# Four orders changed in a fused graph layer: SyncE's stores, two early loads, one edge step, one block's preparation

## The chip, the cores and the metric

The kernel runs on one core of a Trainium2 chip. The metric is the device time of one launch in microseconds (us), here always of the whole program. PE is TensorE, DVE is VectorE, ACT is ScalarE, POOL is GpSimd, and SP is SyncE, which here issues most DMAs. Each engine works through its own instructions in the order in which they are written; semaphores tie the engines together.

## The reference

One layer on N = 6250 nodes with 256 features and E = 206250 edges sorted by their target. Three terms are added to x, and a mixture of experts follows:

```python
xn = layernorm(x)
# graph attention, 8 heads of 32, 4 edge types
feat = xn @ W_n
el, er = einsum('nhd,hdt->nht', feat, attn_l), einsum('nhd,hdt->nht', feat, attn_r)
e = (sum_t(el[src] * mask) + sum_t(er[dst] * mask) + sum_t(em * mask)) / 3
e = where(e > 0, e, 0.2 * e)
a = exp(e - segment_max(e, dst)[dst]); a = a / segment_sum(a, dst)[dst]
gnn = segment_sum(feat[src] * a[:, :, None], dst)
# linear attention over the nodes
q = softmax(q, -1) * scale; k = softmax(k, over nodes)
mix = layernorm_gamma((q @ (k.T @ v)) @ Wout)
x = x + gnn + mix
# 8 experts, each three layers of 256 x 256
w = softmax(mean over batch of xn2 @ Wr + br)      # xn2 = layernorm(x), batch of 1
h = relu(bn(xn2 @ W1[e] + b1)); h = relu(bn(h @ W2[e] + b2)); y = h @ Wo[e] + bo
x = x + sum_e w[e] * y[e]
```

## The kernel before

There are three phases, each a block of the five engines' programs that ends with a barrier.

**The node phase** works on 49 tiles of 128 nodes. It makes the table of features (256 values and 32 logits of each node) that the edges gather from, and the linear attention. POOL first stores the table, then gathers the rows of 26 edge groups (PRE) ahead of the edge phase (`gather_ahead`, L440): each group is eight indirect gathers into one of two halves of `stage`, and a half is free again when SP has stored it (`ahead_out`). SP stores a gathered group with `store_ahead(i)` (L366), which waits for the group's gathers. Its order is written out by hand: the first 11 groups (FIRST_BESIDE), then for each of the seven chunks c of x one group and one `reload(c)` (L378, 896 KB of x, again needed for the residual), then the output loop. There DVE's `finish` (L683) writes output tile t to one of four buffers of `kexp`, and needs the store of tile t - 4 to have landed; SP's `store_mix` (L371) stores it, three tiles later in SP's own count. After tiles t = 5, 11, ..., 47 of SP's count comes one more `store_ahead`, from number EARLY = 18 on. The last store is `store_er` (L382, 1.2 MB), and SP then waits for all landings (L398).

**The edge phase** has 202 groups of 1024 edges, walked in 250 visits (a group beside a target tile), two visits to a step, so steps k = 0 to 124 (K = 125) and two more to drain. POOL gathers the source rows (L972), eight gathers to a group, and tells the group as `ready` when the gathers have landed, four gathers into the next group or at the end. In step k PE turns the logits of k (`turn_logits`, L1302), makes one-hot transposes and edge terms of k + 1, sums the messages of k - 1 (`segment_sums`, L1325, of which the second visit's last five chunks come at the end of the step), adds the gathered terms of k + 1 (`source_terms`, L1292, the only part that waits for `ready`) and turns the running maxima of k (`turn_maxima`, L1312). In step k DVE does two scans of k (L1181, L1186), `logits` of k + 1 (L1108), `differences` of k (L1192, L1194), `over_terms` and `leak` of k + 1 (L1122, L1126), the selection for k + 2, then `absent` (L1130) and the new maxima of k - 1, which need both segment sums of k - 1, and last the messages of k (L1173). SP loads the edge data of step k + 4 and stores the sums. Two loads for the FFN's block 0, `xm` (L945) and `am` (L946), are issued at step K - 1 = 124 of SP's program.

**The FFN phase** has 13 blocks of four or three node tiles and eight experts (x = 0 to 7). `block_of` sets one order for PE, ACT and DVE: in column x come `up` of x + 1, `middle` of x, `down` of x - 1 and one part of the next block's preparation. Its parts are: 0, normalise the sums, add the residual, statistics (DVE); 1, the deviation (ACT) and xn (DVE, L1699 and L1702); 2, transposes (PE, L1796) and a copy (ACT); 3, the router's matmuls (PE, L1804); 4, the router's logits and the splitting of xnT into two parts (DVE); 5, exp (ACT) and the weights (DVE); 6, transposes of the weights (PE, L1810) and their copy wT (DVE, L1739); 7, the bias matmuls (PE, L1816) and the start of y (DVE, L1744). Every fp32 matrix is used as a high and a low part, so each product is three matmuls (L1822 to L1824), and DVE splits h after each relu (L1653, L1655). In block 0 ACT and DVE also split the weights of each expert as they arrive (`cast_weight`, L1588; `weight_rest`, L1659: one rest in `up`, two in `middle`), and the preparation of block 0's own parts 5 to 7 stands in columns 0 and 1.

Of the kernel before, what the change touches and what calls it, by code (L numbers as in the profile page):

```python
# [42 lines left out]
K = V // 2  # L43
SLOTS = 4
GSLOTS = 7
NEAR = 8
PRE = 26
EARLY = 18
FIRST_BESIDE = 11
REST_AFTER = 1  # L50
RESTS = 1
# [15 lines left out]
B = 4  # L67
# [113 lines left out]
def phase_nodes(nc, io, scr, kept_on):  # L181


    with ExitStack() as ctx:
# [129 lines left out]
        def _(sp):  # L314
# [69 lines left out]
            for i in range(FIRST_BESIDE):  # L384
                store_ahead(i)
            for c in range(NT // XC):
                store_ahead(FIRST_BESIDE + c)
                reload(c)
            turns = dict(zip(range(5, NT, 6), range(EARLY, PRE)))
            tiles(sp, (store_mix, 3), unrolled=True, at={t: partial(store_ahead, i) for t, i in turns.items()})  # L390
# [412 lines left out]
def phase_edges(nc, io, scr, kept_on, opening):  # L803


    with ExitStack() as ctx:
# [40 lines left out]
        opening_in = sem("g_opening_in")  # L847
# [55 lines left out]
        def _(sp):  # L903
# [34 lines left out]
            for k in range(SLOTS):  # L938
                loads(k, k)
                if k == 0:  # L940
                    sp.dma_start(idx[:, :], io["src"][:, NEAR * C:]).then_inc(idx_in, 16)

            def load_first_sums():

                sp.dma_start(opening.xm[:, :, :], scr["xmix"][0:B].rearrange("a p c -> p a c")).then_inc(opening_in, 16)  # L945
                sp.dma_start(opening.am[:, :, :], scr["acc"][0:B].rearrange("a p c -> p a c")).then_inc(opening_in, 16)  # L946

            assert (G - 1) + (B - 1) < 2 * (K - 4)

            def step(k, s):  # L950
                if isinstance(k, int) and k == K - 1:
                    load_first_sums()
                if not known(k, 3):
                    store(k - 3, (s + 1) % 2, 1)
                if not (isinstance(k, int) and k + SLOTS >= K):
                    loads(k + SLOTS, s)
                if not (known(k, 2) or isinstance(k, int) and k >= K + 2):
                    store(k - 2, s % 2, 0)
# [122 lines left out]
        def _(dve):  # L1081
# [123 lines left out]
            def step(k, s):  # L1205

                q = s % 2
                alive = not (isinstance(k, int) and k >= K)
                more = not (isinstance(k, int) and k + 1 >= K)
                joining = not known(k, 2)  # L1210
# [6 lines left out]
                    dve.wait_ge(runm_ok, k + 1)  # L1217
                if joining and not (isinstance(k, int) and k >= K + 2):
                    join(k - 2, q, 0)
                if more:  # L1220
                    logits(k + 1, (s + 1) % SLOTS)
                if alive:
                    differences(k, s)
                if more:
                    over_terms(k + 1)
                    leak(k + 1)
                if choosing:
# [20 lines left out]
                if alive:  # L1248
                    messages(k, s, 0, at[0])
                    messages(k, s, 1, at[1])  # L1250

            over_terms(0)
            leak(0)
# [3 lines left out]
        def _(pe):  # L1257
# [79 lines left out]
            def step(k, s):  # L1337
# [15 lines left out]
                    turn_one_hot(k + 1, s1, 1)  # L1353
                if summing:
                    segment_sums(k - 1, s0, 1, range(0, BEFORE))
                if more:
                    source_terms(at, groups)
                if alive:
                    turn_maxima(k, s)
                if summing:  # L1360
                    segment_sums(k - 1, s0, 1, range(BEFORE, C))

# [3 lines left out]
def phase_ffn(nc, io, scr, kept_on, opening):  # L1366
# [4 lines left out]
    with ExitStack() as ctx:  # L1371
# [93 lines left out]
        def halves(n):  # L1465

            return -(-n // 2)

        SHORT = NB * B - NT
        FULL = NB - SHORT  # L1470
        assert SHORT == 3 and FULL % 2 == 0 and FULL * B + SHORT * (B - 1) == NT
# [5 lines left out]
        def blocks(eng, prepare, up, middle, down):  # L1477
# [4 lines left out]
            def block_of(b, s, n, following):  # L1482
                opening = isinstance(b, int) and b == 0
                for x in range(X):
                    if x < X - 1:
                        up(b, s, n, x + 1)
                    elif following:
                        up(b + 1, 1 - s, following, 0)
                    if opening and x < 2:
                        prepare(0, 0, B, 5 + x)  # L1490
                    middle(b, s, n, x)
                    if opening and x == 1:
                        prepare(0, 0, B, 7)
                    if x > 0:
                        down(b, s, n, x - 1)
                    elif not (isinstance(b, int) and b == 0):
                        down(b - 1, 1 - s, B - 1 if isinstance(b, int) and b > FULL else B, X - 1)
                    if following:
                        prepare(b + 1, 1 - s, following, x)

            for x in range(3):
# [466 lines left out]
```

## Time and profile before

| | |
|---|---|
| median of 3 runs | 3161.24 us (3158.49 to 3166.12) |
| the profiled execution | 3170.54 us, its span 3168.9 us |
| PE busy | 2874.6 us, 91% |
| DVE busy | 2638.7 us, 83% |
| POOL busy | 1852.1 us, 58% (all of it before the FFN) |
| ACT busy | 1700.9 us, 54% |
| node phase | to about 367 us |
| edge phase | to about 2257 us |
| FFN phase | the rest |

The shares are means over three phases with different limits, so no one of them tells what an edit is worth. The four edits lie in short stretches: the output loop (263 to 367 us), the last steps of the edge phase (2150 to 2257 us) and block 0 of the FFN (2257 to 2370 us). For each, the timeline of the engines is read together with what ended the idle time before an instruction. Times are us from the span's start.

### The profile page before, as it was taken

Reading aid. Unit: us, or ns where it says so; the run is one execution under the profiler, and the core shown is the slowest. Engines: PE = TensorE matmul, PEld = TensorE weight load, DVE = VectorE, ACT = ScalarE, POOL = GpSimd, SP = SyncE. Lnnn points to the kernel's source line nnn. Section 1 sums busy time; section 2 is a strip of 40 time slices with the busy share of each in tenths; the row PEclk is TensorE's granted clock in tenths of the full one; section 3 lists DMA queues with packets and bytes.
Section 4 is the critical chain, followed back from the end, with each engine's and each line's share of the span. In section 5 each row is a group of like instructions: output and inputs, shape, how many; then the busy total and the mean of one; then the engine's idle time right before and its main releaser. Section 6 shows DMA issues by size and latency. Waiting matters only on the chain. (4 is left out here: it accounts for less than half of the span.)

```text
span 3168.9 us, 76579 instructions
## 1 busy us (share of the span) xinstructions
PE 2874.6 (91%) x21350; PEld 2376.5 (75%) x21351; DVE 2638.7 (83%) x4799; ACT 1700.9 (54%) x5754; POOL 1852.1 (58%) x3341
## 2 busy tenths in 40 slices
PE   8996589998999999999899999898599999999999
PEld 5565377776777777777777777776388888888899
DVE  5676698998999998899999999898587777777776
ACT  5552256665666665666666666665543333333343
POOL 3888688888888888888888888887000000000000
PEclk9998899999999999999999999999799999999999
DMA  8678867676776767676667676665211000000000
GB/s 312 211 252 298 307 193 202 202 208 197 206 212 199 208 195 197 199 206 199 203 196 205 199 207 206 199 203 156 76 52 34 21 22 21 22 21 18 18 23 10
DMA packets 275943, 500.38 MB, mean 158 GB/s; under 512 B 80679, under 2 KB 177474, under 8 KB 269008
## 3 DMA queue, kind: packets, MB, share of 16 engines
q0 software_dynamic: 85456, 282.69, 30.8%
q1 hardware_dynamic: 190336, 215.88, 21.4%
q8 instruction: 69, 1.13, 0.1%
q14 instruction: 82, 0.67, 0.1%
HBM read 410.81 MB, written 87.57 MB: 157 GB/s over the span
## 5 line engine op out<-in xcount | busy, mean ns | idle before, releaser
L972 POOL DMA_INDIRECT gat<-scratch_table,idx x1360 | 1323.6, 973 | 239.0 <-issue 229.9
L1325 PE MATMUL ps_s<-msg,oh 128*128 128x272 f32 x4000 | 1029.0, 406 | 106.0 <-ACT tmp L1038 55.9
L1325 PEld LDWEIGHTS ps_s<-msg,oh 128*128 128x128 f32 x4000 | 742.7, 193 | 255.5 <-ACT tmp L1038 107.6
L1047 ACT ACTIVATE acc<-acc,sc 128x33 f32<-128x33 f32 x2000 | 458.8, 340 | 224.2 <-DVE acc L1161 222.3
L1610 ACT ACTIVATE h<-ps_h,fsh,fsc 128x512 f32<-128x512 f32 (+1 forms) x416 | 291.1, 751 | 508.8 <-PE ps_h L1824 508.8
L1173 DVE TENSOR_TENSOR msg<-gat,ps_m 128x2048 f32<-128x2048 f32 x250 | 559.3, 2277 | 0.0
L1563 POOL DMA_DIRECT2D out<-y x13 | 9.9, 759 | 897.2 <-DVE y L1778 897.2
L1038 ACT ACTIVATE tmp<-ps_s,sc 128x33 f32<-128x33 f32 x2000 | 386.7, 305 | 17.2
L1027 ACT CAST oh<-ps_o 128x1024 f32<-128x1024 bf16 x250 | 259.3, 1037 | 139.2 <-PE ps_o L1264 137.7
L1653 DVE CAST h_hi<-h 128x1024 fp32r<-128x1024 f32 (+1 forms) x208 | 137.2, 660 | 201.9 <-ACT h L1610 201.8
L1186 DVE TENSOR_TENSOR_SCAN runm<-penr,ps_e 16x1024 f32<-16x1024 bf16 x125 | 284.3, 2274 | 12.8
L1181 DVE TENSOR_TENSOR_SCAN ps_e<-penr,ps_e 16x1024 f32<-16x1024 bf16 x125 | 284.5, 2276 | 2.0 <-PE ps_e L1302 2.0
L1655 DVE TENSOR_TENSOR h_lo<-h,h_hi 128x1024 fp32r<-128x1024 f32 (+1 forms) x208 | 242.1, 1164 | 7.2
L440 POOL DMA_INDIRECT stage<-scratch_table,pidx x208 | 205.2, 987 | 43.6 <-issue 41.3
L1822 PE MATMUL ps_y<-w_hi,h_hi 128*128 128x256 f32 x784 | 219.8, 280 | 1.7 <-DVE y L1778 1.7
L1823 PE MATMUL ps_y<-w_lo,h_hi 128*128 128x256 f32 x784 | 220.0, 281 | 0.0
L1824 PE MATMUL ps_y<-w_hi,h_lo 128*128 128x256 f32 x784 | 219.7, 280 | 0.0
L1032 ACT ACTIVATE sc<-dd 128x16 f32<-128x16 f32 x250 | 60.2, 241 | 294.7 <-DVE dd L1155 294.7
L144 POOL MEMSET rest_e<- 128x16 f32 x1408 | 203.7, 145 | 0.4
L1292 PE MATMUL ps_z<-gat,ident 128*128 x500 | 136.8, 397 | 55.6 <-POOLq L992 54.3
L1278 PEld LDWEIGHTS ps_z<-er3e,ohT 128*128 128x128 bf16 x6000 | 168.6, 96 | 18.2 <-issue 0.3
L1264 PE MATMUL ps_o<-identb,ohT 128*128 128x128 bf16 x2000 | 153.7, 220 | 27.3 <-DVE ohT L1101 25.9
(224 smaller groups left out, 5319.8 us busy)
## 6 DMA issues: line engine op xcount, KB each, us to landing
d16r<-scratch_dst SPq DMA_DIRECT2D x250, 256.0 KB
scratch_acc<-acc SPq DMA_DIRECT2D x250, 136.0 KB
scratch_ahead<-stage SPq DMA_DIRECT2D x26, 1152.0 KB, 4.8
gat<-scratch_ahead POOLq DMA_DIRECT2D x26, 1152.0 KB
edge<-in_edge SPq DMA_DIRECT2D x250, 88.0 KB
gat<-scratch_table,idx POOLq DMA_INDIRECT x1360
scratch_table<-stage POOLq DMA_DIRECT2D x49, 144.0 KB, 5.3
xq<-in_xT SPq DMA_DIRECT2D x7, 896.0 KB, 11.4
```

The costliest lines, as they stand in the source:

```text
L972: pool.indirect_dma_start(out=gat[:, s, c, :], out_offset=None, in_=scr["table_rows"], in_offset=bass.IndirectOffsetOnAxis(ap=rows[:, at:a ...
L1027: act.copy(oh[:, s, j, :, :], ps_o[:, 0:C, :]).then_inc(oh_ok, 1)
L1038: act.mul(tmp[:, j, cols], ps_s[j][:, cols], sc[:, j, 1, h:h + 1]).then_inc(tmp_ok, 1)
L1047: act.mul(acc[:, new, cols], acc[:, old, cols], sc[:, j, 0, h:h + 1]).then_inc(scaled, 1)
L1173: dve.tensor_tensor(m4[:, :, :, 0:DH], gat[:, row_of(at), :, 0:D].rearrange("p a c (h d) -> p (a c) h d", h=H), ps_p.rearrange("p (c j h) ...
L1181: dve.tensor_tensor_scan(ps_e[0:2 * H, 0:GE], penr[:, s, 0:GE], ps_e[0:2 * H, 0:GE], NEG, ALU.add, ALU.max).then_inc(runf_ok, 1)
L1186: dve.tensor_tensor_scan(runm[:, ::-1], penr[:, s, GE:0:-1], ps_e[0:2 * H, GE - 1::-1], NEG, ALU.add, ALU.max).then_inc(runm_ok, 1)
L1325: last = pe.matmul(ps_s[j][:, 0:SUMS], oh[:, s, j, c, :], msg[:, 2 * (s % 2) + j, c, :], start=(c == 0), stop=(c == C - 1), skip_group_che ...
L1610: act.activation(hid[:, m, 0:n * P], ps_h[2 * layer + m][:, 0:n * P], ACT.Relu, bias=sh[:, layer, x * KD + m:x * KD + m + 1], scale=sc[:, ...
L1655: dve.tensor_tensor(lo, whole, hi.bitcast(F32), ALU.subtract).then_inc(parts, 1)
L1822: pe.matmul(out, a_hi, b_hi, start=start, stop=False)
L1823: pe.matmul(out, a_hi, b_lo, start=False, stop=False)
```

## The change

- SyncE's stores around the output loop: EARLY is 17. The last chunk's `reload(6)` is no longer preceded by a group's store; group 17 is stored in the output loop after t = 5, groups 18 to 24 after t = 11 to 47, and group 25 after the loop, ahead of `store_er`.
- The early FFN loads: `xm` is issued at step K - 4 = 121 of SP's program, behind the last edge loads and store of step 120, and `am` at step K = 125.
- Step K - 2 = 123 of the edge phase: DVE does `logits`, `over_terms` and `leak` of step 124 at the end, after the messages; PE turns the maxima of step 123 ahead of `source_terms`, while the last five chunks of the segment sums stay behind both.
- Block 1's preparation, which runs in the columns of block 0: part 0 in column 2 (it was in 0), 1 and 2 in column 3, 3 in column 4, 4 in 5, 5 in 6, and 6 and 7 in column 7. Later blocks keep one part to a column.

```diff
@@ -45,7 +45,7 @@
 GSLOTS = 7
 NEAR = 8
 PRE = 26
-EARLY = 18
+EARLY = 17
 FIRST_BESIDE = 11
 REST_AFTER = 1
 RESTS = 1
@@ -384,7 +384,8 @@
             for i in range(FIRST_BESIDE):
                 store_ahead(i)
             for c in range(NT // XC):
-                store_ahead(FIRST_BESIDE + c)
+                if FIRST_BESIDE + c < EARLY:
+                    store_ahead(FIRST_BESIDE + c)
                 reload(c)
             turns = dict(zip(range(5, NT, 6), range(EARLY, PRE)))
             tiles(sp, (store_mix, 3), unrolled=True, at={t: partial(store_ahead, i) for t, i in turns.items()})
@@ -940,15 +941,20 @@
                 if k == 0:
                     sp.dma_start(idx[:, :], io["src"][:, NEAR * C:]).then_inc(idx_in, 16)
 
+            def load_mixed():
+
+                sp.dma_start(opening.xm[:, :, :], scr["xmix"][0:B].rearrange("a p c -> p a c")).then_inc(opening_in, 16)
+
             def load_first_sums():
 
-                sp.dma_start(opening.xm[:, :, :], scr["xmix"][0:B].rearrange("a p c -> p a c")).then_inc(opening_in, 16)
                 sp.dma_start(opening.am[:, :, :], scr["acc"][0:B].rearrange("a p c -> p a c")).then_inc(opening_in, 16)
 
             assert (G - 1) + (B - 1) < 2 * (K - 4)
 
             def step(k, s):
-                if isinstance(k, int) and k == K - 1:
+                if isinstance(k, int) and k == K - SLOTS:
+                    load_mixed()
+                if isinstance(k, int) and k == K:
                     load_first_sums()
                 if not known(k, 3):
                     store(k - 3, (s + 1) % 2, 1)
@@ -1205,6 +1211,7 @@
             def step(k, s):
 
                 q = s % 2
+                closing = isinstance(k, int) and k == K - 2
                 alive = not (isinstance(k, int) and k >= K)
                 more = not (isinstance(k, int) and k + 1 >= K)
                 joining = not known(k, 2)
@@ -1217,11 +1224,11 @@
                     dve.wait_ge(runm_ok, k + 1)
                 if joining and not (isinstance(k, int) and k >= K + 2):
                     join(k - 2, q, 0)
-                if more:
+                if more and not closing:
                     logits(k + 1, (s + 1) % SLOTS)
                 if alive:
                     differences(k, s)
-                if more:
+                if more and not closing:
                     over_terms(k + 1)
                     leak(k + 1)
                 if choosing:
@@ -1248,6 +1255,10 @@
                 if alive:
                     messages(k, s, 0, at[0])
                     messages(k, s, 1, at[1])
+                if closing:
+                    logits(k + 1, (s + 1) % SLOTS)
+                    over_terms(k + 1)
+                    leak(k + 1)
 
             over_terms(0)
             leak(0)
@@ -1353,10 +1364,13 @@
                     turn_one_hot(k + 1, s1, 1)
                 if summing:
                     segment_sums(k - 1, s0, 1, range(0, BEFORE))
-                if more:
+                closing = isinstance(k, int) and k == K - 2
+                if more and not closing:
                     source_terms(at, groups)
                 if alive:
                     turn_maxima(k, s)
+                if closing:
+                    source_terms(at, groups)
                 if summing:
                     segment_sums(k - 1, s0, 1, range(BEFORE, C))
 
@@ -1466,6 +1480,7 @@
 
             return -(-n // 2)
 
+        OPENING = [(), (), (0,), (1, 2), (3,), (4,), (5,), (6, 7)]
         SHORT = NB * B - NT
         FULL = NB - SHORT
         assert SHORT == 3 and FULL % 2 == 0 and FULL * B + SHORT * (B - 1) == NT
@@ -1495,7 +1510,10 @@
                         down(b, s, n, x - 1)
                     elif not (isinstance(b, int) and b == 0):
                         down(b - 1, 1 - s, B - 1 if isinstance(b, int) and b > FULL else B, X - 1)
-                    if following:
+                    if opening:
+                        for part in OPENING[x]:
+                            prepare(1, 1, B, part)
+                    elif following:
                         prepare(b + 1, 1 - s, following, x)
 
             for x in range(3):
```

## Rows read from the trace of the kernel before

**Rows 1.** Timeline, SP's DMA issues: start us, us, queue, line, operation, out<-in, count

```profile
263.73 0.32 SPq L366 DMA_DIRECT2D scratch_ahead<-stage  x1
...
274.32 0.32 SPq L366 DMA_DIRECT2D scratch_ahead<-stage  x1
...
275.19 3.51 SPq L371 DMA_DIRECT2D scratch_xmix<-kexp  x3
...
356.25 0.33 SPq L366 DMA_DIRECT2D scratch_ahead<-stage  x1
...
361.76 0.43 SPq L382 DMA_DIRECT2D scratch_er<-er  x1
```

**Rows 2.** Timeline, DVE in the output loop; the brackets: idle before, releaser

```profile
284.64 0.48 DVE L683 SCALAR_TENSOR_TENSOR kexp<-mixo,rstd,ktile 128x256 f32<-128x256 f32 x1 [14.63 <-DMA scratch_xmix<-kexp]
```

**Rows 3.** Timeline, POOL, the last gather of the node phase

```profile
352.60 0.96 POOL L440 DMA_INDIRECT stage<-scratch_table,pidx  x1 [0.18 <-issue]
```

**Rows 4.** Views of lines 398 and 366, whole run: SP's last waits; landings of group stores

```profile
L398 SPq EVENT_SEMAPHORE  x3: 28/847/2948, 362.2 to 366.1; - x3
...
DMA to landing us min/median/max: 4.1/4.8/6.3
```

**Rows 5.** Timeline, SP, the first of the two early FFN loads

```profile
2204.08 0.43 SPq L945 DMA_DIRECT2D xm<-scratch_xmix  x1
```

**Rows 6.** Timeline, POOL, the last gather of the edge phase

```profile
2203.55 0.95 POOL L972 DMA_INDIRECT gat<-scratch_table,idx  x1 [0.18 <-issue]
```

**Rows 7.** Timeline, PE, steps 123 and 124 of the edge phase

```profile
2210.49 2.07 PE L1292 MATMUL ps_z<-gat,ident 128*128 x4 [8.44 <-POOLq L992]
...
2213.45 4.17 PE L1325 MATMUL ps_s<-msg,oh 128*128 128x272 f32 x10
...
2217.46 1.04 PE L1302 MATMUL ps_e<-ident,e 128*16 128x128 f32 x8
...
2221.18 5.31 PE L1325 MATMUL ps_s<-msg,oh 128*128 128x272 f32 x22 [2.68 <-DVE msg L1173]
...
2228.04 0.64 PE L1312 MATMUL ps_m<-ident,runm 16*128 16x16 f32 x8 [1.55 <-DVE runm L1186]
```

**Rows 8.** Timeline, DVE, steps 123 and 124 of the edge phase

```profile
2212.60 0.75 DVE L1108 TENSOR_TENSOR zm<-ps_z,edge 128x256 f32<-128x256 f32 x2 [9.18 <-PE ps_z L1292]
...
2213.97 0.68 DVE L1122 TENSOR_REDUCE lg<-zm 128x128 f32<-128x512 f32 x1
...
2223.24 2.28 DVE L1181 TENSOR_TENSOR_SCAN ps_e<-penr,ps_e 16x1024 f32<-16x1024 bf16 x1
```

**Rows 9.** Windows: us, busy by engine, then PEclk, DMA share, GB/s

```profile
2206.50:2207.00 0.50, 0.00 (x0) 0.00 (x0) 0.00 (x0) 0.00 (x0) 0.00 (x0) 0.51 0.46 134
```

**Rows 10.** Timeline, PE, block 0 of the FFN

```profile
2300.55 1.22 PE L1816 MATMUL ps_t<-bo_parts,wT 96*128 96x256 f32 x4 [7.30 <-DVE wT L1739]
...
2306.16 0.39 PE L1822 MATMUL ps_h<-fxnT_hi,w_hi 128*128 128x512 f32 x1
...
2314.57 1.04 PE L1796 MATMUL ps_t<-ident,fxn 128*128 128x128 f32 x8
...
2323.87 1.84 PE L1804 MATMUL ps_t<-wr,fxnT 128*128 128x8 f32 x16
```

**Rows 11.** Timeline, DVE, block 0 of the FFN

```profile
2292.25 0.18 DVE L1671 TENSOR_SCALAR rs<-am 128x32 f32<-128x32 f32 x1
...
2297.08 0.38 DVE L1686 BATCH_NORM_AGGREGATE fmv<-fst 128x2 f32<-128x6 f32 x4
...
2307.36 1.39 DVE L1702 TENSOR_SCALAR fxn<-x,fmv,fsd 128x256 f32<-128x256 f32 x4
...
2313.54 0.69 DVE L1653 CAST h_hi<-h 128x1024 fp32r<-128x1024 f32 x1 [0.34 <-ACT h L1610]
...
2315.41 1.29 DVE L1659 TENSOR_TENSOR w_lo<-w_raw,w_hi 128x512 fp32r<-128x512 f32 x2
...
2316.61 1.65 DVE L1778 SCALAR_TENSOR_TENSOR y<-ps_y,w,y 128x256 f32<-128x256 f32 x4
```

## The prediction

> **What bounds the kernel now.** The three phases stand one behind another, so I read each place that the change touches by itself: the page's slices to see the phases, then the waits of each stretch, the timeline of each engine there, and the granted clock. The node phase ends with SP's queue: stores of gather groups, stores of output tiles and one last store share it, and its end is 366.1 us [rows 1, 4]. The edge phase's last steps are one chain through TensorE (PE) and VectorE (DVE), fed by POOL's gathers. In the FFN, PE is the bound once block 0 is past; inside block 0 it waits for DVE once, until 2300.55 [rows 10].
>
> **Part 1, the order of SyncE's stores.** Before, SP issues reload 5 right after the store of group 16 (issued 263.73), then waits for gather group 17 (274.32), and only then come reload 6 and the first output tile's store (275.19) [rows 1]. DVE stands 14.63 us, until 284.64, for that store to free its buffer [rows 2]. After, reload 6 and output stores 0 to 2 go ahead of group 17's store, so store 0 is issued near 265 instead of 275.2. It has two reloads and a group store in front of it on the DMA rings and lands, by the 9.4 us that the old one took behind one of each, some 10 to 12 us later: 275 to 277.5. DVE thus runs 7 to 9 us ahead. That gain doesn't reach the end of the phase. POOL's gathers run without a break and end at 352.60 + 0.96 = 353.56; the store of the last group goes out at 356.25 [rows 1, 3], and that is a floor. In the new order this store comes behind all output stores, and the store of er behind it. Before, er's store goes out at 361.76 and the phase ends at 366.1, 4.3 us later [rows 1, 4]. After, both go out at 356.3 and 356.7; a group's store lands 4.8 us after issue [rows 4], and er's bytes (as many again) behind it need about 3 us: 364.1. Gain 2.0 us. Against it: group 17's store now has reload 6 in front, and gather group 19 waits for it. Before, it had some 2 us to spare (274.32 + 5 against the start of group 19 near 281.3, counted back from 353.56 by seven groups of 10.3 us, eight gathers of 0.96 us with their gaps and fills each); reload 6 in front costs 0 to 3.5 us of landing, so POOL loses 0 to 1.5 us, and all that follows on POOL with it. I take 0.8. **Part 1: -1.2 us**, bounds -3 (the rings clear faster than 4.8 us a store) to +2 (POOL loses 3.5 and only 1.5 is saved).
>
> **Part 2, the early FFN loads.** xm (512 KB) and am (544 KB) are issued from 2204.08 on, while POOL's last gather is issued at 2203.55 and over by 2204.5 [rows 5, 6]. PE waits until 2210.49 for it (8.44 us idle) [rows 7]: 5.9 us from issue to use. In the node phase the last gather of group 25 was in use 356.25 - 353.56 = 2.7 us after issue [rows 1, 3]. Without the two loads beside it I take 2.7 us: ready at 2207.2, 3.2 us sooner. xm now goes out behind step 120's loads, near 2167, beside gathers of that time; each group's landing is awaited by POOL only after four more gathers (5 us), and even the 5.9 us seen here would cost POOL 0.9 us, so 0 to 0.9, taken 0. am goes out after the last loads, near 2228, ahead of the store of visit 245; nothing needs either before the phase's end, 26 us later. No cost.
> The Trainium skill says in DMA: Bandwidth & Descriptors, section Queues, rings and completion order, that each DMA engine takes turns between the queues it has work for. By that rule two busy queues halve each other; the trace agrees (5.9 against 2.7 us). It speaks against the earlier xm as well: gathers beside it would take twice as long, which by the four gathers' margin is still hidden.
>
> **Part 3, the last step but one.** In step 123 PE now turns the maxima before it waits for the gathers, and DVE puts logits, over_terms and leak of step 124 behind the messages. What is queued where decides. PE's remaining segment sums of visit 245 are still behind source_terms, and DVE's absent() still waits for those sums, ahead of the messages. So the wait for the gathers reaches the messages as before, less only the 0.96 us that turning the maxima took between them. The row: source_terms 2210.49, sums from 2213.45 for 4.17 [rows 7]; so from ready to the end of the sums 7.1 us, after 6.2. From the end of the sums to the next scan DVE takes 2223.24 - 2217.62 = 5.6 us [rows 7, 8]. New on the path behind that: logits 0.75, over_terms 0.68 and the short leak, with gaps 1.8 us [rows 8], then PE's turning of the logits, 1.04 us at near full clock [rows 7] and up to 2.1 at half. Before, all of it lay beside the sums, hidden.
> The clock: in PE's idle time, which began at 2202.0, the granted clock was at 0.51 by 2206.5, the level of 1.2 GHz [rows 9], so source_terms took 2.07 us and ten matmuls 4.17, against 22 in 5.31 at full clock (0.24 each) [rows 7]. Now the pause is some 3.5 us, from the maxima near 2203.7 to 2207.2, and then there is a second one of over 7 us, while DVE does messages and logits. I take the low clock for both: 2207.2 + 6.2 = 2213.4 sums; + 5.6 = 2219.0; + 1.8 = 2220.8; turning 1.8 = 2222.7. PE then has 22 matmuls of step 123 that ran before 2226.5 [rows 7] and now start at 2222.7: ten at 0.42 and twelve at 0.24, 7.1 us, to 2229.8; the scans (4.7 us) end earlier, 2227.4. The maxima of step 124, before at 2228.04 [rows 7], come at 2229.8, and the rest of the phase is one chain from there. **Parts 2 and 3: +1.8 us.** Bounds: the clock still up at 2207.2 gives sums at 2210.9, maxima at 2227.3, -0.7; the gathers no sooner than before gives +5.0, with POOL's 0.9 +5.9. Alone, part 2 would have given some -5 and part 3 takes it.
>
> **Part 4, block 1's preparation.** DVE's part 0 runs from 2292.25 to 2297.46, 5.2 us, ahead of the copy of wT for which PE waits until 2300.55 [rows 10, 11]. Moved behind, PE goes on at 2295.5: -5.1. The pause shrinks from 7.3 to 2.3 us, so the down matmuls keep the full clock: the matmuls from 2300.55 to 2306.16 took 5.6 us [rows 10], at full clock 3.3, another -2.3. So up(3) starts at 2298.8, 7.4 us sooner.
> Then the work comes back. PE needs 8.41 us for a weight column x (2306.16 to 2314.57) [rows 10] and would reach the transposes, now at the end of x = 3, after two columns, at 2298.8 + 16.8 = 2315.6. They need part 1 from DVE, and DVE works in order through all of its x = 2 and x = 3 first. That is twice: two splits of 1.87 (2313.54 to 2315.41), three weight rests of 0.6 (two from 2315.41 to 2316.61), four updates of y in 1.6 [rows 11], 7.2 us; and once part 0 with 5.2 and part 1 with 1.6 (1.39 and its reciprocal) [rows 11]: 21.2 us. It can start when ACT hands over the first relu of x = 2, 4.5 us after up(3) starts (2.8 of matmuls, 1.4 of relu, hops): 2303.3, and it waits 0.5 us for the other relu: 2325.0. So PE waits 9.4 us, and comes back at half clock. Place by place: up(5) started at 2306.16 + 16.8 + 0.8 for the transposes + 1.7 for the router's matmuls (2323.87) [rows 10] = 2325.5. Now: 2325.0 + 1.5 for slow transposes = 2326.5, +1.0; the router's 1.7 are still to come, +1.7; and up(5) itself at half clock, by the 2.3 us saved above less the transposes' 0.7, +1.6. At the end of x = 7 parts 6 and 7 stand together: after middle(7) DVE needs ACT's relu 1.5, the split 1.87, four y updates 1.6 and the copy of wT 0.6, 5.7 us with hops, while PE has 2.8 of down matmuls and 0.45 of transposes: it waits 2.5 before the bias matmul, where before a whole column lay between. In all +1.0 + 1.7 + 1.6 + 2.5 = 6.8; less 0.3 for a short old wait for a weight rest. **Part 4: +6.5 us.** Bounds +3 (half the second wait hidden) to +9 (the clock falls in the 2.3 and 2.6 us pauses too). Other loads: am and xm of block 2 wait for part 0, 14 us later than before and still 60 us early.
>
> **Sum.** -1.2 + 1.8 + 6.5 = +7.1 us, on an execution of 3170.54 us (span 3168.9): 0.22%. The same on the median of 3161.24 gives 3168.3. That execution is 9 us above the median; nothing above depends on it.
>
> **Rivals.**
> 1. DVE keeps up in block 0 (the not slower side). If part 0 found free time on DVE in column 2, PE would wait at the transposes only for the last y updates and part 1, 2.7 us, at full clock, and part 4 would be -7.4 + 2.7 + 2.5 = -2.2: total -1.6, 3159.6. It decides at 16.8 us of PE against 21.7 of DVE. For it: DVE has idle pieces in the old columns (0.34 before 2313.54) [rows 11]. Against: the count above leaves it none. 0.13.
> 2. The clock is up at 2207.2: -0.7 instead of +1.8, total +4.6, 3165.8, no difference that can be told. For it: the pause is shorter than the 4.5 us in which the clock fell. 0.17.
> 3. The 14.63 us stall was on the path: the phase ends with DVE, 6 us sooner. Against: the floor at 356.25. -6 instead of -1.2: 3163.5. 0.08.
> 4. The change doesn't do what it says with the gathers: they land as late without the loads. +5.0 instead of +1.8: 3171.5. Against: they share the rings from 2204.5 to 2210.5. 0.15.
> The forecast 0.42; the rest, POOL's loss and falls of the clock in the short pauses, 0.05, above it.
>
> **Chances.** About 0.2% (6.3 us, 3167.6) is what can be told from no change. The forecast lies just over it: three quarters of its case slower. Slower 0.49, same 0.43, faster 0.08 (most of rival 1's and 3's lower ends). The range for 8 in 10: 3161.0, between rivals 1 and 3, to 3174.0, rival 4 with part 4's upper bound.
>
> **What would show it.** Output loop: DVE's wait shrinks to some 5 us, and POOL's last gather ends at 353.6 to 355; the edge phase starts under 2 us sooner. Step 123: source_terms near 3 us sooner after the last gather, a PE gap of 7 us before the logits are turned, half clock after it. Block 0: bias matmul 5 us sooner, a gap of 9 us before block 1's transposes, one of 2 to 3 before its bias matmul. Wrong if no such 9 us gap is there, or if the node phase is shorter by over 4 us.

## The result

The changed kernel takes 3169.42 us (median of 11 runs, 3166.18 to 3176.59); the kernel before, measured beside it, takes 3161.24 us (3157.93 to 3167.98). The ratio is 1.0027, with a 95% interval from 1.0018 to 1.0036: 8.5 us slower, between 5.7 and 11.4. The prediction was 3168.3 us. All medians are over all launches; the ratios leave out the few launches that were far slower than their fellows.

The profiled execution's span is 3174.9 us, where the one of before is 3168.9. The busy times of the page hardly move, so the stretches have to be read one by one. In this section line numbers are those of the changed kernel.

**The output loop.** SP's DMA issues (timeline: start, duration, queue, line, operation, out<-in, count), the counterpart of [rows 1]:

```profile
261.98 0.32 SPq L366 DMA_DIRECT2D scratch_ahead<-stage  x1
262.39 1.61 SPq L378 DMA_DIRECT2D ktile<-in_x  x2
264.06 2.70 SPq L371 DMA_DIRECT2D scratch_xmix<-kexp  x3
274.79 0.33 SPq L366 DMA_DIRECT2D scratch_ahead<-stage  x1
...
356.29 0.33 SPq L366 DMA_DIRECT2D scratch_ahead<-stage  x1
356.66 0.43 SPq L382 DMA_DIRECT2D scratch_er<-er  x1
366.46 0.37 SPq L909 DMA_DIRECT2D edge<-in_edge  x1
```

The last line is the edge phase's first load; before it stood at 369.26. The waits of POOL and DVE there (engine, tile and line, releaser: us in total, times, longest):

```profile
POOL stage L441 <- DMA scratch_ahead<-stage: 4.1, 3, 2.1
...
DVE kexp L684 <- DMA scratch_xmix<-kexp: 7.2, 2, 6.9
```

DVE's stall of [rows 2] is halved. POOL's wait for group stores is new: between 200 and 360 us no wait of POOL with that releaser stands in the kernel before, nor in the three other profiles of the old order.

**The end of the edge phase.** PE, the counterpart of [rows 7] (brackets: idle before, releaser):

```profile
2205.72 2.07 PE L1303 MATMUL ps_z<-gat,ident 128*128 x4 [5.25 <-POOLq L998]
2207.58 4.11 PE L1336 MATMUL ps_s<-msg,oh 128*128 128x272 f32 x10
2219.16 1.88 PE L1313 MATMUL ps_e<-ident,e 128*16 128x128 f32 x8 [7.47 <-DVE e L1132]
2220.82 7.06 PE L1336 MATMUL ps_s<-msg,oh 128*128 128x272 f32 x22
2227.82 0.67 PE L1323 MATMUL ps_m<-ident,runm 16*128 16x16 f32 x8
```

POOL's last gather is issued at 2200.26 and over at 2201.21, so source_terms waits 4.5 us for its landing, where it was 5.99. DVE, the counterpart of [rows 8]:

```profile
2211.72 0.17 DVE L1136 TENSOR_SCALAR absn<-ps_s 128x16 f32<-128x16 f32 x1 [9.19 <-PE ps_s L1336]
...
2212.91 4.48 DVE L1179 TENSOR_TENSOR msg<-gat,ps_m 128x2048 f32<-128x2048 f32 x2
2217.30 0.75 DVE L1114 TENSOR_TENSOR zm<-ps_z,edge 128x256 f32<-128x256 f32 x2
...
2221.07 2.28 DVE L1187 TENSOR_TENSOR_SCAN ps_e<-penr,ps_e 16x1024 f32<-16x1024 bf16 x1 [1.97 <-PE ps_e L1313]
```

Both new pauses are there: absent waits 9.19 us for sums that stand behind source_terms, and PE waits 7.47 us until the logits are made, then turns them in 1.88 us instead of 1.04.

**Block 0 of the FFN.** PE, the counterpart of [rows 10]:

```profile
2293.67 0.74 PE L1834 MATMUL ps_t<-bo_parts,wT 96*128 96x256 f32 x4 [2.19 <-DVE wT L1757]
...
2297.07 0.39 PE L1840 MATMUL ps_h<-fxnT_hi,w_hi 128*128 128x512 f32 x1
...
2323.03 1.94 PE L1814 MATMUL ps_t<-ident,fxn 128*128 128x128 f32 x8 [8.98 <-DVE fxn L1720]
...
2364.20 0.99 PE L1834 MATMUL ps_t<-bo_parts,wT 96*128 96x256 f32 x4 [2.42 <-DVE wT L1757]
```

The wait for wT falls from 7.30 to 2.19 us, up(3) starts at 2297.07, and then come the waits of 8.98 and 2.42 us that weren't there. Block 1's bias matmul, before which PE now stands 2.42 us, had no wait in the kernel before:

```profile
2360.05 0.64 PE L1816 MATMUL ps_t<-bo_parts,wT 96*128 96x256 f32 x4
```

Where they leave the FFN is read from block 2's copy of wT, which comes once in each block; here the kernel before and then the changed one:

```profile
2424.35 0.68 DVE L1739 CAST wT<-ps_t 96x512 fp32r<-96x512 f32 x1
```

```profile
2430.16 0.68 DVE L1757 CAST wT<-ps_t 96x512 fp32r<-96x512 f32 x1
```

From the FFN's first DVE instruction (2257.09 and 2255.66) that is 167.26 and 174.50 us: the FFN loses 7.2 us in its first two blocks, and from there both kernels run alike (744.6 and 744.7 us to the end of the span).

### The profile page after: what moved, and what is told of

Its sections match the earlier page's. It is cut to its first block and busy times, and to the rows that moved or that the text cites. A ratio compares the mean times of both kernels' runs of the same rounds, so it can differ in the third digit from the quotient of the medians.

```text
span 3174.9 us, 76579 instructions
## 1 busy us (share of the span) xinstructions
PE 2879.9 (91%) x21350; PEld 2381.7 (75%) x21351; DVE 2637.6 (83%) x4799; ACT 1697.8 (53%) x5754; POOL 1846.5 (58%) x3341
## 5 line engine op out<-in xcount | busy, mean ns | idle before, releaser
L1044 ACT ACTIVATE tmp<-ps_s,sc 128x33 f32<-128x33 f32 x2000 | 384.4, 304 | 17.2
L441 POOL DMA_INDIRECT stage<-scratch_table,pidx x208 | 205.0, 985 | 47.4 <-issue 41.0
## 6 DMA issues: line engine op xcount, KB each, us to landing
xq<-in_xT SPq DMA_DIRECT2D x7, 896.0 KB, 10.2
```

Of the source, the lines that this page charges most:

```text
L1044: act.mul(tmp[:, j, cols], ps_s[j][:, cols], sc[:, j, 1, h:h + 1]).then_inc(tmp_ok, 1)
```

## The experiments

Part 1 is the order of SP's stores, part 2 the early FFN loads, part 3 step 123, part 4 block 1's preparation. Twelve experiments ran, each with a profile and each timed beside the kernel before; e3b_p2 and e4b_p1 are the kernels of e3_p2 and e4_p1 once more. Those of the first group (e1_p4, e2_p23, e3_p2, e4_p1) and the third (e4b_p1, e6_late, e7_map) ran on chips on which the first two phases take some 1350 to 1400 us longer, whatever the kernel (the kernel before has medians of 4556.78 and 4507.98 us there). There the FFN can be read as elsewhere, the two other places only with care. The second group (e5_p3, e3b_p2, e8_sums, e9_er) and e10_all ran on chips like the first (3161.89 and 3161.29 us).

The times alone can't resolve single parts, so each part is read by a count inside the profile, from a fixed point just ahead of it to one just behind it:

| count, us | old order | changed kernel |
|---|---|---|
| store of group 16 to the edge phase's first load | 105.5, 104.7, 106.0, 105.1: mean 105.4 | 104.5 |
| store of group 16 to the end of POOL's last gather | 89.8, 89.3, 90.3, 90.9: mean 90.1 | 92.2 |
| end of the last edge gather to the FFN | 52.6, 51.5: mean 52.1 | 54.5 |
| FFN's start to block 2's wT | nine executions, 164.6 to 167.4 (eight of them from 166.4): mean 166.8 | 174.5 |

Each entry is one execution, so a difference inside the scatter of its row shows nothing.

**e1_p4: part 4 alone.**

```diff
+        OPENING = [(), (), (0,), (1, 2), (3,), (4,), (5,), (6, 7)]
...
+                    if opening:
+                        for part in OPENING[x]:
+                            prepare(1, 1, B, part)
```

> Part 4 alone: block 1's preparation in the new columns, all else as in the kernel before. Theory: DVE falls behind in column 2 and PE pays it back twice, so the FFN shows the gap of some 9 us ahead of block 1's transposes and one of 2.4 us ahead of its bias matmul, and is 6.5 to 7.5 us longer than before: about 3168 us where the kernel before has 3161. Rival (DVE keeps up in block 0, the gap is due to the late start of the edge phase's end or to something else in the changed kernel): the FFN is some 2 us shorter, 3159, and no such gap is there. The part is additive if the FFN's length is the changed kernel's (919.3 us) within 0.5.

Measured: ratio 1.0016 (1.0001 to 1.0031). PE's waits in block 0:

```profile
3689.76 0.74 PE L1820 MATMUL ps_t<-bo_parts,wT 96*128 96x256 f32 x4 [2.23 <-DVE wT L1743]
3719.14 1.94 PE L1800 MATMUL ps_t<-ident,fxn 128*128 128x128 f32 x8 [8.99 <-DVE fxn L1706]
```

Block 2's wT comes 174.2 us after the FFN's start, 7.4 later than the old mean; the FFN is 918.5 us long, 0.7 from the changed kernel's 919.2 and so just outside the 0.5 that was set for "additive"; by the count to block 2's wT the two are 0.3 apart. The part shows nearly its whole size alone, and the rival falls.

**e2_p23: parts 2 and 3 together**, as in the diff above.

> Parts 2 and 3 together: the two early loads moved, and step 123 reordered. Theory: the gathers are in use 1.4 us sooner after the last issue, and the logits, their terms and the turning that were hidden beside the segment sums now stand on the chain, so the stretch from scan 123 to the barrier is 1.8 us longer than before, and the whole about 2 us or 0.06% slower, too little to tell from the times but to be read from the spans of the stages. Rival (the gathers land as late as before): 5 us longer. Rival (the changed kernel's edge phase differs only because its POOL started elsewhere): the stretch is as long as before, within 0.5 us.

Measured: ratio 1.0012 (0.9995 to 1.0029). On this chip POOL's last gather (issued 3564.9) had landed long before step 123, so source_terms never waited, and the run measures part 3 for a case that I hadn't costed:

```profile
3599.90 2.45 PE L1335 MATMUL ps_s<-msg,oh 128*128 128x272 f32 x10
3609.82 1.88 PE L1312 MATMUL ps_e<-ident,e 128*16 128x128 f32 x8 [7.47 <-DVE e L1131]
3611.49 6.58 PE L1335 MATMUL ps_s<-msg,oh 128*128 128x272 f32 x22
```

The same pause of 7.47 us. From scan 123 to the FFN's start it takes 52.2 us, where the six kernels of this kind of chip with the old step 123 take 46.0 to 47.5 (e4_p1 47.4): part 3 costs 4.7 to 6.2 us when nothing is late, not the 1.8 expected for the two parts. The logits, their terms and their turning then stand on the chain with no late landing to pay for them.

**e3_p2: part 2 alone.**

```diff
+            def load_mixed():
...
-                if isinstance(k, int) and k == K - 1:
+                if isinstance(k, int) and k == K - SLOTS:
+                    load_mixed()
+                if isinstance(k, int) and k == K:
                     load_first_sums()
```

> Part 2 alone: the two early loads moved, step 123 as before. Theory A (the loads share the rings with the last gathers): source_terms starts some 4.5 us after the last gather's issue has ended, where before it was 5.9, and since step 123 waits for just that, the edge phase ends 1.4 us sooner, up to 3 us if the pause gets short enough for the granted clock to stay up. Theory B (the prediction's own number, 2.7 us after the issue): 3.2 us sooner at the least and some 5 with the clock. Rival (the loads are innocent, and the gathers take 5.9 us anyway): no change. And if xm beside the gathers of step 121 costs POOL something, the last gather ends later than before by up to 0.9 us.

Measured: ratio 0.9986 (0.9970 to 1.0002), with PE not waiting for the gathers at all (source_terms starts 17.2 us after the last of them). Nothing follows for the landing; the same kernel ran again as e3b_p2.

**e4_p1: part 1 alone**, EARLY 17 and the skipped group store.

> Part 1 alone: the new order of SyncE's stores. Theory: the phase's end is set by the last group's store behind POOL's last gather, with er's store right behind it, so the first load of the edge phase goes out near 366.5 where before it was 369.3, 2.8 us sooner, of which the prediction had 1.2. Of the 8 us by which DVE runs ahead nothing else arrives. The whole is 2.8 us or 0.09% faster. Rival (DVE's 14.6 us stall was on the path): some 6 us sooner. Rival (POOL's gathers lose by it): the last gather of the phase ends over 1.5 us later and the gain is gone.

Measured: ratio 1.0016 (1.0000 to 1.0033). On this chip POOL waits 145.5 to 155.0 us for group stores in the node phase with the old order (three kernels), and 159.7 with the new one. The first load of the edge phase stands at 547.31, where those three have 533.89 to 539.59: 8 to 13 us later, not 2.8 sooner. With one execution on a chip where POOL waits so long for stores, that is no size for part 1 elsewhere.

**e5_p3: part 3 alone**, without the moved loads.

> Part 3 alone: step 123 reordered, the two loads where they were. Where the last gathers are on time, parts 2 and 3 together showed a pause of 7.47 us before the logits are turned and 4.8 us more from the sums of step 123 to the barrier. Theory (the pause of PE is what part 3 costs, the landing what part 2 gives): with the gathers landing 5.9 us after the last issue, as in the kernel before, this kernel's stretch from the last gather's issue to the barrier is 3 to 5 us longer than before, and its source_terms start as late as before. Rival (part 3 hides the pause behind the gathers' landing, as it may be meant to): no longer than before, within 0.5 us. Where the gathers are on time, both kernels show the same 4.8 us.

Measured: 3165.15 us, ratio 1.0007 (0.9998 to 1.0016).

```profile
2198.50 2.07 PE L1297 MATMUL ps_z<-gat,ident 128*128 x4 [6.40 <-POOLq L992]
2200.36 4.42 PE L1330 MATMUL ps_s<-msg,oh 128*128 128x272 f32 x10
2212.25 1.88 PE L1307 MATMUL ps_e<-ident,e 128*16 128x128 f32 x8 [7.47 <-DVE e L1126]
2213.91 7.22 PE L1330 MATMUL ps_s<-msg,oh 128*128 128x272 f32 x22
```

From the last gather's end (2192.84) to source_terms 5.7 us, as with the old order, and 56.1 us to the FFN, 4.0 more than the old mean. The theory holds in this profile, and the rival, that the reorder hides the landing, falls: the pause ahead of source_terms is still 6.40 us, and one of 7.47 is added.

**e3b_p2: part 2 alone again.**

> Part 2 alone once more, beside part 3 alone, for a run in which POOL's last gathers are the late ones. Theory A (the loads share the rings with the last gathers): source_terms starts some 4.5 us after the last gather's issue has ended instead of 5.9, and the edge phase ends 1.4 us sooner, or up to 3 if the granted clock stays up in the shorter pause. Rival (the loads are innocent): no change. Where the gathers are on time and PE doesn't wait for them: no change by either.

Measured: 3162.30 us, ratio 0.9997 (0.9988 to 1.0005).

```profile
2204.86 2.07 PE L1297 MATMUL ps_z<-gat,ident 128*128 x4 [6.81 <-POOLq L997]
...
2215.94 8.36 PE L1330 MATMUL ps_s<-msg,oh 128*128 128x272 f32 x22 [2.68 <-DVE msg L1178]
```

4.4 us from the last gather's end (2200.47) to source_terms: the landing is 1.2 us sooner, by theory A, not the prediction's 3. Only 0.5 of it arrives (51.6 us to the FFN against 52.1), less than the 1.1 us between the two executions of the old order: the 22 matmuls behind the pause took 8.36 us, most of it at the low level (granted clock 0.50 from 2216 to 2222, 0.96 in the two us behind), where [rows 7] has 5.31.

**e8_sums: parts 2 and 3, with the last segment sums of step 123 ahead of source_terms.** Against the changed kernel:

```diff
+                if summing:
+                    segment_sums(k - 1, s0, 1, range(BEFORE, C))
                 if closing:
                     source_terms(at, groups)
-                if summing:
-                    segment_sums(k - 1, s0, 1, range(BEFORE, C))
```

> Parts 2 and 3 with one difference: in step 123 PE does its last ten matmuls of the segment sums ahead of source_terms, so that DVE's absent and the messages no longer wait for the gathers. Theory (the sums queued behind source_terms are what makes part 3 dear): absent starts some 9 us sooner than in the changed kernel, the messages and the logits follow, the gathers' landing lies beside the messages, and the edge phase ends some 8 us sooner than the changed kernel's where the gathers are late (6 to 7 us sooner than before). Rival (DVE's own chain of messages, logits, terms and leak is the bound of the step): no more than 2 us sooner than the changed kernel. Where the gathers are on time, the order of the sums costs nothing either way, and it takes as long as parts 2 and 3 together, within 1 us.

Measured: 3156.03 us, ratio 0.9981 (0.9973 to 0.9990). PE, and then DVE:

```profile
2200.17 1.75 PE L1302 MATMUL ps_z<-gat,ident 128*128 x4 [2.55 <-POOLq L997]
2205.09 1.88 PE L1312 MATMUL ps_e<-ident,e 128*16 128x128 f32 x8 [3.16 <-DVE e L1131]
```

```profile
2197.66 0.17 DVE L1135 TENSOR_SCALAR absn<-ps_s 128x16 f32<-128x16 f32 x1 [0.46 <-PE ps_s L1335]
...
2198.84 4.48 DVE L1178 TENSOR_TENSOR msg<-gat,ps_m 128x2048 f32<-128x2048 f32 x2
```

Absent's wait falls from 9.19 to 0.46 us: it comes 1.8 us after the last gather's end (2195.88), where the changed kernel has 10.5. The messages now run while the gathers land. From the last gather's end to the FFN 45.8 us, 8.6 less than the changed kernel and 6.2 less than the old order. What made part 3 dear where the gathers are late was ten matmuls standing behind the one wait of the step. The logits are still made after the messages, 7.5 us behind the end of the sums, but now the landing falls into that time. Two cases weren't run: this order on a chip where the gathers are on time (e2_p23 shows the cost of late logits there, 4.7 us or more), and the sums ahead of source_terms with DVE's old order, in which `logits` stands ahead of the messages and waits for source_terms itself ([rows 8]: 9.18 us).

**e9_er: part 1 with er's store inside the output loop**, after SP's t = 38. Against part 1 alone:

```diff
-            tiles(sp, (store_mix, 3), unrolled=True, at={t: partial(store_ahead, i) for t, i in turns.items()})
+            tiles(sp, (store_mix, 3), unrolled=True, at={t: partial(store_ahead, i) for t, i in turns.items()} | {38: store_er})
...
-            store_er()
```

> Part 1 with one more move: er's store goes into the output loop, after SP's t = 38, so that the last group's store is the last thing on the ring. Theory (the last group's store sets the end, and er's 1.2 MB behind it cost the rest): the first load of the edge phase goes out 2.3 us sooner than in part 1 alone, 5.1 us sooner than before: the node phase ends with that store's landing, 4.8 us after its issue. Rival (er's bytes cost the same wherever they stand, since the stores of the loop wait for them): no gain over part 1, and the last group's store goes out later by up to 3 us.

Measured: 3161.03 us, ratio 0.9997 (0.9988 to 1.0005).

```profile
356.01 0.33 SPq L366 DMA_DIRECT2D scratch_ahead<-stage  x1
364.48 0.37 SPq L908 DMA_DIRECT2D edge<-in_edge  x1
```

From the last group's store to the first load 8.5 us instead of 10.2: 1.7 saved of 2.3. But POOL's last gather ends 92.7 us after the store of group 16, so only 0.8 us of it arrives (103.7 against 104.5). Without the count nothing could be said: the first load stands at 364.48 here, and at 364.64 in e5_p3, with the old order.

**e4b_p1: part 1 alone again.**

> Part 1 alone once more, beside kernels whose node phase is undisturbed. Counted from the store of group 16, the kernels with the old order (four profiled executions) took 104.7 to 106.0 us to the edge phase's first load and 89.3 to 90.9 us to POOL's last gather; the changed kernel took 104.5 and 92.2. Theory (two terms that nearly cancel: POOL loses some 2 us, since group 17's store lands later, and SP's tail gives 3 back): 104.5 within 0.5 and 92.2 within 0.7 again; the whole is at most 1 us faster than before, 0.03%. Rival (part 1 is worth the 2.8 us that the two first profiles show): 102.5 to 103 us and POOL's last gather at 90.

Measured: ratio 1.0011 (0.9996 to 1.0027), on a chip of the other kind: first load at 531.70, where two kernels with the old order have 532.58 and 533.25, and POOL waits 153.6 us for group stores (147.1 and 146.4). POOL's stalls for its stores fill the stretch there and the expected count isn't comparable, so this run decides nothing; that part 1 brings no more than a microsecond rests on the counts in the table and on e9_er.

**e6_late: part 0 in column 2, the transposes one column later.**

```diff
+        OPENING = [(), (), (0,), (1,), (2,), (3, 4, 5), (6,), (7,)]
```

> The kernel before with another map for block 1's preparation: part 0 in column 2 and part 1 in column 3 as in the changed kernel, but the transposes one column later (4), parts 3, 4 and 5 in column 5, part 6 in 6, part 7 in 7. Theory (the loss of part 4 is PE waiting at block 1's transposes while DVE is behind, and at the bias matmul with parts 6 and 7 in one column): the 9 us gap ahead of the transposes goes and the 2.4 us gap too, so what is left is the gain at wT; the FFN is 4 to 6 us shorter than before, some 906 us against 911 (mean of eight old ones, 908 to 914), the changed kernel's 919. Rival (DVE's 5.2 us for part 0 are paid in block 0 wherever they stand, since DVE has no free time there): PE waits for the relu's splits instead, and the FFN is 911 or longer.

Measured: ratio 0.9994 (0.9978 to 1.0010).

```profile
3640.89 1.22 PE L1820 MATMUL ps_t<-bo_parts,wT 96*128 96x256 f32 x4 [2.20 <-DVE wT L1743]
3665.51 0.79 PE L1826 MATMUL ps_h<-fxnT_hi,w_hi 128*128 128x512 f32 x1 [2.74 <-DVE w_lo L1663]
3676.77 1.04 PE L1800 MATMUL ps_t<-ident,fxn 128*128 128x128 f32 x8
```

Both gaps are gone, as expected, but block 2's wT comes at 166.8 us, exactly the old mean, and the FFN is 910.7 us long: no gain, where 906 was expected. DVE's timeline shows why: the splits of the relu stand behind part 0's last instruction, and the weight rest behind them.

```profile
3662.64 0.38 DVE L1690 BATCH_NORM_AGGREGATE fmv<-fst 128x2 f32<-128x6 f32 x4
3662.93 0.66 DVE L1657 CAST h_hi<-h 128x1024 fp32r<-128x1024 f32 x1
...
3664.77 0.68 DVE L1663 TENSOR_TENSOR w_lo<-w_raw,w_hi 128x512 fp32r<-128x512 f32 x1
```

PE waits 2.74 us, and the granted clock is 0.52 and 0.50 in the six us from 3664.6 on. It was 0.54 behind the wait at wT too, and that part of the miss isn't the map's: up(3) starts 43.2 us after the FFN's start here and 41.2 in e1_p4, which is the same code up to there, so some 2 of the missing 4.7 us are a fall of the clock that the one kernel had and the other hadn't. So the rival was half right: the rest of the miss is part 0's place in column 2.

**e7_map: part 0 in column 1.**

```diff
+        OPENING = [(), (0,), (1,), (2,), (3, 4), (5,), (6,), (7,)]
```

> The kernel before with part 0 in column 1, part 1 in column 2, the transposes in column 3, parts 3 and 4 in column 4, then 5, 6 and 7 each in a column of its own. Theory (each part wants one column between DVE's or ACT's work and PE's use of it, and part 0 only has to leave the copy of wT free): the stall at wT shrinks and no other appears; the FFN is 5 to 6 us shorter than before, 905 to 906 us. Rival (column 1 is as bad as column 0, for block 0's own parts 5 to 7 stand there): the stall at wT stays 7 us and the FFN is as long as before, 911.

Measured: ratio 0.9972 (0.9958 to 0.9986).

```profile
3634.44 0.75 PE L1820 MATMUL ps_t<-bo_parts,wT 96*128 96x256 f32 x4 [2.20 <-DVE wT L1743]
3647.97 0.50 PE L1826 MATMUL ps_h<-fxnT_hi,w_hi 128*128 128x512 f32 x1 [1.54 <-DVE w_lo L1663]
3656.49 1.04 PE L1800 MATMUL ps_t<-ident,fxn 128*128 128x128 f32 x8
```

Block 2's wT at 161.0 us, 5.8 sooner than the old mean; the FFN is 904.9 us long, as expected, and the rival falls. The wait at the weight rest is 1.54 us and the clock stays at 1.00 through it. The ratio says 12.6 us (6 to 19) of 4508, so the profile's 6 lies at its lower end.

**e10_all: all four, mended** (e9_er, e8_sums and e7_map together).

> All four orders, mended: part 1 with er's store inside the output loop; parts 2 and 3 with the last ten matmuls of the segment sums of step 123 ahead of source_terms; part 4 with the map of the run with part 0 in column 1. Theory (the stages add up): node phase 1.6 us shorter counted from the store of group 16 (103.7 against 105.3), the stretch from POOL's last gather to the FFN 6.3 us shorter (45.8 against 52.1), block 2's copy of wT 6.0 us sooner after the FFN's start (161 against 166.9). In all 13.9 us less than before, 0.44%, about 3147.5 where the kernel before has 3161.5, and 22 less than the changed kernel. Rival (the stages don't add: an earlier end of one shifts the next into a worse place, as an earlier FFN start does to the loads of the weights): under 10 us. Where POOL's gathers aren't the late ones at the end of the edge phase, the middle term is 4 to 5 us of loss instead and the whole is 3 us or less.

Measured: 3149.57 us where the kernel before has 3161.29, ratio 0.9966 (0.9953 to 0.9978). Node phase 104.9 us (0.4 less than the old mean, not 1.6: POOL's wait for group stores is 4.9 us here); last gather's end to the FFN 45.5, 6.6 less; block 2's wT at 161.4, 5.4 less. Together 12.4 us, measured 11.7, expected 13.9; the rival (under 10 us) falls by the median, though the interval reaches from 7 to 15 us. By the two ratios it is some 19 us ahead of the changed kernel; the two weren't timed beside each other. Its wait at wT ended as in e6_late:

```profile
2278.76 1.22 PE L1833 MATMUL ps_t<-bo_parts,wT 96*128 96x256 f32 x4 [2.20 <-DVE wT L1756]
```

The granted clock is 0.50 in the 2.2 us behind it, and up(3) starts at 43.1 us after the FFN's start where e7_map has 41.3, but block 2's wT comes only 0.4 us later than there: with part 0 in column 1 the fall of the clock hardly costs anything.

## Why the prediction was right, point by point

**Part 1 (predicted -1.2): the sum held within the scatter, both terms were too small.** The two profiles side by side say -2.8 us (369.26 to 366.46), but the four of the old order lie between 364.6 and 369.3, so that difference is mostly where POOL's gathers happened to be. By the counts it is -0.9, one execution against four that lie within 1.3 us, so its size is hardly more than its noise. POOL loses 2.1 us (0.8 predicted; 4.1 us of waiting in three places), because group 17's store and the ones after it come later; from POOL's last gather to the first load 3.0 are saved (12.3 against a mean of 15.3; 2.0 predicted). Rival 3 falls: DVE's stall went from 14.63 to 6.9 us, and 6 us at the end of the phase didn't follow.

**Parts 2 and 3 (predicted +1.8): measured +2.4** against the mean of the old order, +1.9 between the two profiles. That the sum came out so near is luck: it holds sizes that were off and cancel. The landing was taken as 2.7 us, from a wait of SP in the node phase; at the end of the edge phase it is 4.5, 4.4, 4.3 and 4.6 us in the four kernels with the moved loads, and 6.0, 5.3 and 5.7 in three with the old ones. So the loads cost the gathers 1.2 us, not 3.2: the landing is some 27% longer beside them and not twice as long, so the reading by which two busy queues halve each other isn't borne out, and 5.9 against 2.7 us was no evidence for it, since the two rows came from different phases. Why the gathers of the node phase land sooner isn't shown. By rival 4 the landing would have stayed at 5.9, and it didn't, though it stayed nearer to that than to 2.7. Against it, the last 32 matmuls took 9.29 us instead of the 10.51 of before, which is the granted clock and not the change (e9_er, with the old order, has 9.29 too), and the terms between came out some 0.5 us shorter. The rest is as written: a pause of 7.47 us (over 7), turning at 1.88 (1.8), 22 matmuls 7.06 (7.1), and the claim that part 3 takes back what part 2 gives. But alone they are -0.5 and +4.0, where some -5 and +6.8 were predicted: part 2's own size was off by 4.5 us, and part 3's by 2.8 the other way.

**Part 4 (predicted +6.5): measured +7.2 against the profile of before, +7.7 against the mean of nine.** Step by step: up(3) 7.7 us sooner (7.4); wait at the transposes 8.98 (9.4); up(5) at 69.0 us after the FFN's start, where before it was 68.5 (+0.5, predicted +1.0); wait at the bias matmul 2.42 (2.5), reached 5.6 us later than before (108.5 against 103.0). What was missing is behind it: in the 2.42 us pause the granted clock falls too (the first matmuls after it start 0.43 us apart, where in the fast stretch behind 2297.07 it is 0.23), and the last 1.7 us arise between there and block 2's wT. The upper bound had this in it, the value didn't. That the clock stays up in the 2.3 us pause at wT, worth 2.3 us in the sum, held in three executions of five (e6_late and e10_all have it fall). Rival 1 falls with e1_p4, and e6_late shows in DVE's timeline that it has no room in column 2.

**Sum.** By the counts -0.9 + 2.4 + 7.7 = +9.2 us; predicted +7.1; measured +8.5 (5.7 to 11.4). Most of it is part 4, whose mechanism was right and whose size was nearly so. Rival 2, the clock still up behind the shorter pause, happened in none of the kernels with the old place of the sums: wherever PE waited for the gathers, source_terms took 2.07 us.

## What to carry to other kernels

A wait that can't be avoided belongs behind everything on its engine that others wait for: on top of parts 2 and 3, moving ten matmuls ahead of source_terms gave 8.6 us where the gathers are late, and turned a loss of 2.4 us into a gain of 6.2. Work that is moved off one stall has to be put where its engine has room, which a count of that engine's instructions in the new column tells before any run; a free column for the consumer alone (e6_late) doesn't help. And when two profiles differ by 3 us in a stretch, look at a few more of the old kernel before the difference is explained: measured from a fixed point just ahead of the edit, the scatter here fell from 4.6 to 1.3 us.

## What was not expected of the hardware

- The granted clock after a pause of about 2.2 us isn't the same in each execution: behind the wait at wT the bias matmul took 0.74 or 0.75 us in the changed kernel, e1_p4 and e7_map, and 1.22 in e6_late and e10_all, where the granted clock behind it was 0.54 and 0.50 (1.00 in the changed kernel and e7_map). The same 22 matmuls of step 123 took 5.31 us in one execution of the old order, 7.00 in another (e9_er) and 8.36 in e3b_p2. A single profile's microsecond or two there is not the edit's.
- On two chips the first two phases took some 1350 to 1400 us longer. In the edge phase DVE's `logits` there waits 962 to 1061 us (91 to 100 times) for a releaser that the trace can't name ("remote"); in the kernel before its largest group of waits in the edge phase is 56.5 us. What slows these chips is open. There POOL waits some 150 us for group stores in the node phase, and part 1 came out at 1.0016 (1.0000 to 1.0033) and 1.0011 (0.9996 to 1.0027), where e9_er, which holds it, has 0.9997 elsewhere. An order of stores may be neutral on one chip and dear on another, but that isn't shown: the intervals reach 1.0000, and in e4b_p1 the first load goes out 1 us sooner than with the old order.
